# The last two attention turns written out as one sequence with PSUM banks of their own, and the row work of the last three groups placed behind single feed-forward blocks

## The chip, the core and the metric

The kernel runs on one core of a Trainium2 chip. The metric is the time of one execution on the device in microseconds. Five engines work side by side, each with its own queue of instructions: TensorE (PE in the profile, its weight loads PEld), VectorE (DVE), ScalarE (ACT), GpSimd (POOL) and SyncE (SP), which only starts transfers here. They wait for each other through semaphores written by hand. All five queues are written out in the code; no scheduler reorders them.

## The reference, cut to what matters

64 sequences of 128 rows with 256 features go through two layers:

```
x = x + mlstm(layernorm(x), ctx, ctx, gates...)    # 4 heads; decay matrix D from cumulated gates
x = x + einsum('bsi,oi->bso', layernorm(x), ternary(W0) * scale)
x = x + softmax(layernorm(x) @ Wq @ K.T / 16) @ V  # cross attention on ctx
x = x + bitlinear(silu(bitlinear(n, w_gate)) * bitlinear(n, w_up), w_down)   # n = layernorm(x), inner size 1024
# mlstm: C = (q k.T / 8) * D;  h = (C / norm(C)) @ v, then a normalisation over each head
# bitlinear(a, w): each row of a is rounded to 8 bits by its own absolute maximum; w is ternary
```

## The kernel before

**Groups and two phases.** The 64 sequences form `NG` = 16 groups of `GB` = 4. The first phase, called attention here, takes a group through the first three lines of the reference. The second phase is the feed-forward, the fourth line: 64 blocks of one sequence each.

**Attention.** `schedule` writes out turns. In a turn five groups are at different stages: group n is read in and projected, m = n - 1 goes through the mLSTM (to x1), z = n - 2 through the W0 product and the cross attention (x1 to x2 to x3), y = n - 3 gets its layernorm and rounding factors for the feed-forward, and w = n - 4 is rounded to integers and stored to `rows_q` in DRAM. On TensorE the order within a turn is that of `STAGES`. The names used below: DX (decay exponents), QK, T1 (transpose of x1), F0 (x1 times W0), UA and UB (C times v, called U together), T2 (transpose of x2), SC (scores), WT (transpose of the exponentials), O (weights times V). Each use of a stage takes the next of 8 PSUM banks in a ring (`Banks`); `full[k]` and `clear[k]` count the fillings and emptyings of bank k. The last two turns, `NEXT` and `LAST`, have no group to read in: in `NEXT` m = 15, z = 14, y = 13, w = 12; in `LAST` only z = 15, y = 14 and w = 13 are left. On each engine a turn is one call of `turn`, in a fixed order of steps.

**VectorE in these turns.** `cut_product` multiplies QK by D, `statistics(i, ...)` is four bn_stats, four bn_aggr and a variance (i = 1 for x1, 2 for x2, 3 for x3), the head sums end in `hv`, GpSimd raises to the power -1/2 (`power`, and for the heads L993), and VectorE scales the heads and adds x. `row_steps` takes a group's row maxima (`famax`), its scales and the factors `back`.

**Between the phases.** TensorE, ScalarE and GpSimd wait for `phase1`, which VectorE and ScalarE raise behind their last turn. SyncE starts the transposing reads of `rows_q` for blocks 0 to 3 after the store of group 14, and then four loads of x3 (`fx`).

**Feed-forward.** For block i TensorE does gate_up (L640, eight products of 512 columns), then `product_rows` of block i - 2 (L649) and `down` of block i - 3 (L657). ScalarE does Silu (L878), the copy of the transposed rows (L882) and the scaling out (L889). VectorE multiplies (L1327, output C), takes the row maximum (L1330) and two small steps. GpSimd rounds (L1018) and adds x (L1026). `feed_forward` writes out groups 0 to 2 and 11 to 15; groups 3 to 10, that is blocks 12 to 43, are a loop of two passes. The row work of group 15 is done by `last_rows(i)`, single instructions behind single blocks: on VectorE its row maxima behind blocks 6 to 9, scales and factors behind 10 and 11; on ScalarE the normalisation behind 2 to 5 and the rounding behind 48 to 53.

## Time and profile before

| | us |
|---|---|
| median of 3 runs | 716.62 |
| lowest, highest | 715.96, 718.27 |
| the profiled execution | 717.83 |
| its span, first to last instruction | 716.09 |
| mean granted TensorE clock, share of full | 0.973 |

The profile shows one execution. Its time is 1.2 above the median, and 1.7 of it lie outside the span. Times in the text are microseconds from the start of the span. A row gives the start, the length, the engine, the line in the kernel and the tiles; a group of several instructions has one row, and its length is from the start of the first to the end of the last.

### The profile page before, as it was taken

The page shows a single profiled execution, that of the slowest core. Times are in us where ns is not written, and L with a number is a line of the kernel's source. Part 1 is how long each engine was busy: PE and PEld are TensorE (multiplying, and loading weights), DVE is VectorE, ACT ScalarE, POOL GpSimd, SP SyncE. Part 2 cuts the span into 40 slices and gives each one's busy share as a digit, 9 for nine tenths or more (in the row PEclk, how much of TensorE's full clock was granted, in tenths as well). Part 3 has the DMA queues.
Part 4 walks back from the last instruction along what each step waited for, and adds up shares of the span by engine and source line. Part 5 has one row for each costly group of instructions (what it writes and reads, how often), then busy time and mean ns, then how long its engine had stood idle before and what let it go on. Part 6 is the DMA issues. An engine that isn't in the chain of part 4 may idle for free.

```text
span 716.1 us, 15477 instructions
## 1 busy us (share of the span) xinstructions
PE 674.2 (94%) x4914; PEld 518.3 (72%) x4942; DVE 615.9 (86%) x1654; ACT 515.6 (72%) x1171; POOL 376.9 (53%) x554
## 2 busy tenths in 40 slices
PE   4899999999999999999999999987799999999996
PEld 3687887887977878879779788765365666666664
DVE  4697798898898988988988989887699999999994
ACT  3456576777777768777777687665588887888985
POOL 2253464643834645537346455441266666666665
PEclk9969999999999999999999999988699999999999
DMA  8202022022121220320212202005222332424321
GB/s 302 82 1 60 22 68 90 16 90 77 42 90 45 75 89 16 97 89 23 90 45 75 89 16 74 32 15 161 71 82 83 104 114 81 139 81 139 95 78 60
DMA packets 72653, 55.46 MB, mean 77 GB/s; under 512 B 20093, under 2 KB 72318, under 8 KB 72582
## 3 DMA queue, kind: packets, MB, share of 16 engines
q1 hardware_dynamic: 64134, 50.37, 22.6%
q10 hardware_dynamic: 8448, 4.20, 2.0%
q8 instruction: 38, 0.62, 0.4%
q14 instruction: 33, 0.27, 0.1%
HBM read 29.39 MB, written 20.97 MB: 70 GB/s over the span
## 4 chain that ended last, share of the span: by engine, by line
PE 66%; DVE 20%; ACT 9%; issue 3%; DMA 1%; POOL 0%; DVEq 0%; POOLq 0%; ACTq 0%
PE bank L640 10%; PE bank L556 9%; PE bank L586 8%; PE bank L605 8%; PE bank L657 5%; DVE C L1327 4%; PE bank L626 4%; PE bank L462 4%; DVE hmax L1330 4%; ACT ew L851 4%; PE bank L559 3%; PE bank L525 3%; PE bank L649 3%; PE bank L516 2%; PE bank L598 2%
## 5 line engine op out<-in xcount | busy, mean ns | idle before, releaser
L640 PE MATMUL bank<-WGU,fqT 128*128 128x512 bf16 x484 | 124.5, 389 | 6.7 <-DVEq L1304 3.1
L962 POOL TENSOR_SCALAR_AFFINE_SELECT D<-D 128x512 f32<-128x512 f32 x64 | 38.3, 635 | 158.0 <-ACT D L794 158.0
L640 PEld LDWEIGHTS bank<-WGU,fqT 128*128 128x128 bf16 x512 | 48.4, 99 | 61.1 <-DVE C L1327 17.3
L1327 DVE SCALAR_TENSOR_TENSOR C<-bank,fback,D 128x1024 f32<-128x1024 f32 x64 | 82.1, 1283 | 10.3 <-ACT D L878 6.3
L947 POOL TENSOR_TENSOR rs<-ve,minus_half 128x4 f32<-128x4 f32 x64 | 64.2, 1010 | 50.6 <-DVE ve L1072 50.5
L878 ACT ACTIVATE D<-bank,fback 128x1024 f32<-128x1024 f32 x64 | 71.2, 1113 | 19.1 <-PE bank L640 18.9
L1330 DVE TENSOR_REDUCE hmax<-C 128x1 f32<-128x1024 f32 x64 | 78.1, 1220 | 2.2
L882 ACT ACTIVATE fhT<-bank 128x1024 f16<-128x1024 f16 x64 | 65.5, 1023 | 17.0 <-PE bank L649 16.0
L556 PE MATMUL bank<-WX,qcT 128*128 128x268 f32 x256 | 77.3, 426 | 0.0
L1018 POOL TENSOR_SCALAR wtmp<-C,hscale 128x1024 f32<-128x1024 f32 x64 | 71.6, 1118 | 0.2 <-ACT nrm L889 0.2
L1066 DVE BATCH_NORM_STATS2 st<-x 128x6 f32<-128x256 f32 x192 | 67.2, 411 | 2.9
L657 PE MATMUL bank<-WD,fhT 128*128 128x256 f16 x512 | 66.4, 273 | 0.3 <-ACT fhT L882 0.3
L586 PEld LDWEIGHTS bank<-vaug,C 128*128 128x128 f32 x512 | 62.5, 196 | 2.3 <-issue 1.5
L586 PE MATMUL bank<-vaug,C 128*128 128x65 f32 x512 | 62.3, 276 | 1.4 <-DVE C L1165 1.4
L525 PE MATMUL bank<-qcT,GT 128*128 128x512 f32 x128 | 60.2, 594 | 0.7 <-ACT GT L842 0.7
L605 PE MATMUL bank<-W0T,x1T 128*128 128x256 f32 x256 | 59.4, 385 | 0.1
L993 POOL TENSOR_TENSOR hr<-hv,minus_half 128x16 f32<-128x16 f32 x16 | 47.4, 2960 | 18.0 <-DVE hv L1211 18.0
L1011 POOL TENSOR_SCALAR hback<-hstep,mean_abs 128x1 f32<-128x1 f32 x64 | 17.1, 267 | 74.0 <-DVE hscale L1340 65.0
L605 PEld LDWEIGHTS bank<-W0T,x1T 128*128 128x128 f32 x256 | 47.3, 190 | 9.1 <-DVE C L1165 3.0
L805 ACT ACTIVATE qn<-xg,shift,rs 128x256 f32<-128x256 f32 x64 | 33.2, 589 | 27.9 <-POOL shift L954 27.9
L969 POOL TENSOR_TENSOR hh<-us,head_scale 128x256 f32<-128x256 f32 x64 | 43.9, 705 | 15.6 <-ACT usq L779 15.6
L783 ACT ACTIVATE vg<-bank 128x268 f32<-128x268 f32 x64 | 23.5, 389 | 38.4 <-PE bank L559 38.4
(181 smaller groups left out, 1582.0 us busy)
## 6 DMA issues: line engine op xcount, KB each, us to landing
out_dram<-x SPq DMA_DIRECT2D x32, 512.0 KB, 3.1
xg<-in_x_dram SPq DMA_DIRECT2D x16, 512.0 KB, 3.9
cg<-in_ctx_dram SPq DMA_DIRECT2D x16, 512.0 KB, 4.1
rows_q<-fq ACTq DMA_DIRECT2D x16, 256.0 KB, 2.3
xg<-out_dram SPq DMA_DIRECT2D x8, 512.0 KB, 4.3
cg<-out_dram SPq DMA_DIRECT2D x8, 512.0 KB, 4.4
raw<-in_L_ffn_w_gate_dram SPq DMA_DIRECT2D x1, 1024.0 KB, 8.5
x<-in_L_ffn_w_up_dram SPq DMA_DIRECT2D x1, 1024.0 KB, 10.4
```

The lines of the kernel that those rows point to most:

```text
L525: mm = pe.matmul(o[:, :], GT[:, c, rows_at * P:(rows_at + 1) * P], turned[:, EC + c, :, :].rearrange("p b t -> p (b t)"), start=(c == 0), ...
L556: pe.matmul(o[:, 0:VG], qcT[p][:, EC + c, b, :], WX[:, c, :], start=(c == 0), stop=False, skip_group_check=True)
L586: mm = pe.matmul(o[:, h * AUG:(h + 1) * AUG], C[:, b, h, :], vaug[q][:, b, h, :], start=True, stop=True)
L605: mm = pe.matmul(o[:, 0:E], x1T[:, b, c * P:(c + 1) * P], W0T[:, c, :], start=(c == 0), stop=(c == EC - 1))
L640: mm = pe.matmul(ps[k + half], fqT[:, s, c, :], WGU[:, c, which, half * 512:(half + 1) * 512], start=(c == 0), stop=(c == EC - 1))
L657: mm = pe.matmul(o[:, 0:E], fhT[:, s % 2, c * P:(c + 1) * P], WD[:, c, :], start=(c == 0), stop=(c == IC - 1))
L878: act.activation(fsil[:, s % 2, :], gate, ACT.Silu, scale=fback[:, p, s % FB, 0:1]).then_inc(g_clear, 1)
L882: act.activation(fhT[:, s % 2, :], bank_h[s % 2], ACT.Copy, bias=-OFFSET).then_inc(h_clear, 1)
L1018: pool.tensor_scalar(fhr[:, s % 2, :], fh[:, s % 2, :], hscale[:, s % FB:s % FB + 1], CODE, ALU.mult, ALU.add).then_inc(f_hr, 1)
L1066: dve.bn_stats(st[i][:, b, :], src[:, b, :]).then_inc(stats[i], 1)
L1327: dve.scalar_tensor_tensor(out=fh[:, s % 2, :], in0=up, scalar=fback[:, p, s % FB, 1:2], in1=fsil[:, s % 2, :], op0=ALU.mult, op1=ALU.mult ...
L1330: dve.tensor_reduce(hmax[:, s % FB:s % FB + 1], fh[:, s % 2, :], AX.X, ALU.max, apply_absolute_value=True).then_inc(f_hm, 1)
```

## The change

`Banks` is kept for the first 14 turns. For the last two there is `Places`, which gives each stage banks by name, four for group 14's late stages and four for group 15's:

```diff
+def last_places():
+    start = len(FIRST) + len(SECOND) + (NG - 2) * len(BODY)
+    count = [sum(1 for i in range(start) if i % BANKS == k) for k in range(BANKS)]
+    one, two = (3, 4, 5, 6), (7, 0, 1, 2)
+    a = Places({"TB": (5,), "DX": (6, 7, 0, 1), "MB": (2,), "QK": (3, 4, 5, 6), "T1": two, "UA": (3, 4), "UB": (5, 6),
+                "F0": two, "T2": one, "SC": one, "WT": one, "O": one}, count)
+    b = Places({"T1": two, "F0": two, "T2": two, "SC": two, "WT": two, "O": two}, count)
+    return a, b
```

`fore` is the first of the two, `aft` the second. The two turns are gone from `schedule`; behind it each engine has them written out, and `phase1` is gone. x2 and x3 of group 15 have tiles of their own (`x2_last` = hh, `x3_last` = qn), and the feed-forward's banks are others (gate 3 and 4, up 5 and 6, transposes 7 and 0, down 1 and 2). TensorE:

```diff
-            pe.wait_ge(phase1, 2)
+            turn(fore.part("TB", "DX", "MB", "QK", "T1", "UA", "UB", "F0", "T2", "SC"),
+                 None, NG - 1, NG - 2, None, None, 0, NG % 3)
+            turn(aft.part("T1", "F0"), None, None, NG - 1, None, None, 1, (NG + 1) % 3)
+            turn(fore.part("WT"), None, None, NG - 2, None, None, 0, NG % 3)
+            turn(aft.part("T2", "SC"), None, None, NG - 1, None, None, 1, (NG + 1) % 3)
+            turn(fore.part("O"), None, None, NG - 2, None, None, 0, NG % 3)
+            turn(aft.part("WT"), None, None, NG - 1, None, None, 1, (NG + 1) % 3)
+            pe.wait_ge(x3_ready, GB * (NG - 1))
+            gate_up(0, 0, 0)
+            turn(aft.part("O"), None, None, NG - 1, None, None, 1, (NG + 1) % 3)
...
+                    if i == 2:
+                        pe.wait_ge(x3_ready, GB * NG)
```

VectorE (the steps are the old ones as functions), ScalarE and GpSimd:

```diff
+            cut_product(fore, NG - 1, 0)
+            cut_product(fore, NG - 1, 1)
+            statistics(3, x3, NG - 3)
+            head_sums(fore, NG - 1, 1)
+            x2_rows(fore, NG - 2, x2)
+            moved(fore, "F0", GB - 1)
+            statistics(2, x2, NG - 2)
+            heads_out(NG - 1, 1)
+            dve.wait_ge(x1_ready, NG)
+            statistics(1, x1, NG - 1)
+            row_maxima(fore, NG - 2)
+            scales(0, 0)
+            x2_rows(aft, NG - 1, x2_last)
+            moved(aft, "F0", GB - 1)
+            inverse(fore, NG - 2)
+            statistics(2, x2_last, NG - 1)
+            row_maxima(aft, NG - 1)
+            x3_rows(fore, NG - 2, x2, x3)
...
+            turned_copies(fore, "T2", x2T)
+            turned_copies(aft, "T1", x1T)
+            exponentials(fore, NG - 2)
+            turned_weights(fore)
+            turned_copies(aft, "T2", x2T)
+            exponentials(aft, NG - 1)
+            turned_weights(aft)
+            act.preload_act_table_set("silu_and_others")
...
+            head_power(NG - 1)
+            power(2, NG - 2)
+            power(1, NG - 1)
+            power(2, NG - 1)
```

The row work of groups 13, 14 and 15 goes to `last_rows(i)`, behind single blocks. On ScalarE: rounding of 13 behind blocks 7 to 12, normalisation of 14 behind 14 to 17, its rounding behind 24 to 29, the same for 15 behind 31 to 34 and 41 to 46. On GpSimd: power and shifts of 14 behind block 12, of 15 behind block 29. On VectorE:

```diff
+                if i == 0:
+                    inverse(aft, NG - 1)
+                    x3_rows(aft, NG - 1, x2_last, x3_last)
+                for group, src, at in ((NG - 3, None, 1), (NG - 2, x3, 7), (NG - 1, x3_last, 24)):
+                    if src is not None:
+                        if at <= i < at + GB:
+                            row_statistics(src, i - at)
+                        if i == at + GB:
+                            row_variance(group)
+                        at += 11
+                    if at <= i < at + GB:
+                        row_max(group, (i - at,))
+                    if i == at + GB:
+                        row_scales(group)
+                    if i == at + GB + 1:
+                        row_back(group)
```

The feed-forward has no loop any more, and SyncE's order is another:

```diff
-            for g in range(3):
-                static(g)
-            with eng.Fori(0, NG // 4 - 2) as j:
-                for p in range(4):
-                    turn(4 * j + p + 3, (p + 3) % 4, False, False)
-            for g in range(NG - 5, NG):
-                static(g)
+            for g in range(NG):
+                turn(g, g % 4, g == 0, g == NG - 1)
...
             store(NG - 4)
             store(NG - 3)
-            store(NG - 2)
...
+            sp.wait_ge(q_out, 16 * (NG - 3) + 16)
+            for b in range(FB):
+                rows_turned(b, b)
             sp.wait_ge(x1_ready, NG)
             sp.wait_ge(vaug_ready, GB * NG)
+            sp.wait_ge(x_out, 16 * (NG - 2))
             for g in range(4):
                 sp.dma_start(fx[g], grp(out, g)).then_inc(f_in[g], 16)
-            store(NG - 1)
+            store(NG - 2)
+            sp.wait_ge(x3_ready, GB * NG)
+            sp.dma_start(grp(out, NG - 1), x3_last[:, :, :]).then_inc(x_out, 16)
```

TensorE before, from F0 of group 14 (L605) to O of group 15; L586 is U, L598 are T1 and T2, L613 SC, L621 WT, L626 O:

```order
L605 MATMUL bank<-W0T,x1T 128x256 x8
L586 MATMUL bank<-vaug1,C 128x65 x16
L598 MATMUL bank<-ident,x23 128x128 x8
L613 MATMUL bank<-keyT0,x2T 128x128 x8
L621 MATMUL bank<-ident,ew 128x128 x4
L626 MATMUL bank<-vg2,ewT 128x256 x4
L598 MATMUL bank<-ident,x1 128x128 x8
L605 MATMUL bank<-W0T,x1T 128x256 x8
L598 MATMUL bank<-ident,x23 128x128 x8
L613 MATMUL bank<-keyT1,x2T 128x128 x8
L621 MATMUL bank<-ident,ew 128x128 x4
L626 MATMUL bank<-vg0,ewT 128x256 x4
```

The same place after the change; L615 is U, L634 F0, L627 T1 and T2, L642 SC, L650 WT, L655 O, L666 gate_up of block 0:

```order
L615 MATMUL bank<-vaug1,C 128x65 x16
L634 MATMUL bank<-W0T,x1T 128x256 x8
L627 MATMUL bank<-ident,x23 128x128 x8
L642 MATMUL bank<-keyT0,x2T 128x128 x8
L627 MATMUL bank<-ident,x1 128x128 x8
L634 MATMUL bank<-W0T,x1T 128x256 x8
L650 MATMUL bank<-ident,ew 128x128 x4
L627 MATMUL bank<-ident,hh 128x128 x8
L642 MATMUL bank<-keyT1,x2T 128x128 x8
L655 MATMUL bank<-vg2,ewT 128x256 x4
L650 MATMUL bank<-ident,ew 128x128 x4
L666 MATMUL bank<-WGU,fqT 128x512 x8
```

U stands ahead of F0, WT and O of group 14 moved behind T1, F0 and the scores of group 15, and gate_up of block 0 stands ahead of O of group 15.

VectorE before, from the row maxima of the scores of group 15 to its product of block 1 (C):

```order
L1249 TENSOR_REDUCE rawmax<-bank 128x1 x4
L1253 TENSOR_TENSOR negmax<-rawmax,rs2 128x4
L1283 RECIPROCAL einv<-esum 128x4
L1289 SCALAR_TENSOR_TENSOR x23<-bank,einv,x23 128x256 x4
L1066 BN_STATS st3<-x23 128x6 x4
L1069 BN_AGGR mv3<-st3 128x2 x4
L1072 TENSOR_SCALAR ve3<-mv3 128x4
L1309 COPY fback<-back 128x8
L1327 SCALAR_TENSOR_TENSOR C<-bank,fback,D 128x1024
L1330 TENSOR_REDUCE hmax<-C 128x1
L1337 TENSOR_SCALAR hstep7<-hmax 128x1
L1340 RECIPROCAL hscale<-hstep7 128x1
```

And after the change; L1323 writes x3 of group 14 (x23) and of group 15 (qn):

```order
L1298 TENSOR_REDUCE rawmax<-bank 128x1 x4
L1302 TENSOR_TENSOR negmax<-rawmax,rs2 128x4
L1323 SCALAR_TENSOR_TENSOR x23<-bank,einv,x23 128x256 x4
L1470 SCALAR_TENSOR_TENSOR C<-bank,fback,D 128x1024
L1473 TENSOR_REDUCE hmax<-C 128x1
L1480 TENSOR_SCALAR hstep7<-hmax 128x1
L1483 RECIPROCAL hscale<-hstep7 128x1
L1315 RECIPROCAL einv<-esum 128x4
L1323 SCALAR_TENSOR_TENSOR qn<-bank,einv,hh 128x256 x4
L1470 SCALAR_TENSOR_TENSOR C<-bank,fback,D 128x1024
```

x3 of group 15 stands behind block 0, and its statistics are gone from here. They stand, on VectorE after the change, behind blocks 24 to 28; for group 14 behind blocks 7 to 11, of which this is the end (the single behind block 10, block 11, the aggregations behind it, the product of block 12):

```order
L1167 BN_STATS st3<-x23 128x6
L1470 SCALAR_TENSOR_TENSOR C<-bank,fback,D 128x1024
L1473 TENSOR_REDUCE hmax<-C 128x1
L1480 TENSOR_SCALAR hstep7<-hmax 128x1
L1483 RECIPROCAL hscale<-hstep7 128x1
L1172 BN_AGGR mv3<-st3 128x2 x4
L1174 TENSOR_SCALAR ve3<-mv3 128x4
L1470 SCALAR_TENSOR_TENSOR C<-bank,fback,D 128x1024
```

Before, what stands behind blocks 10 and 11 are the scales and factors of group 15, five small instructions.

## Rows read from the trace of the kernel before

**Rows 1.** The page: busy us (share) xinstructions; then the chain by engine.
```profile
PE 674.2 (94%) x4914; PEld 518.3 (72%) x4942; DVE 615.9 (86%) x1654; ACT 515.6 (72%) x1171; POOL 376.9 (53%) x554
...
PE 66%; DVE 20%; ACT 9%; issue 3%; DMA 1%; POOL 0%; DVEq 0%; POOLq 0%; ACTq 0%
```

**Rows 2.** Windows: length, then busy PE, PEld, DVE, ACT, POOL, clock, DMA share, GB/s.
```profile
500.00:520.00 20.00, 15.34 (x63) 6.60 (x65) 13.63 (x29) 10.07 (x12) 5.46 (x9) 0.66 0.29 89
...
640.00:700.00 60.00, 59.55 (x460) 38.87 (x466) 55.65 (x83) 51.39 (x65) 40.66 (x60) 1.00 0.32 95
```

**Rows 3.** The same view in windows of 4 us.
```profile
476.00:480.00 4.00, 2.75 (x12) 1.99 (x10) 3.40 (x13) 2.61 (x9) 2.02 (x1) 0.50 0.00 0
...
508.00:512.00 4.00, 3.08 (x8) 0.98 (x8) 2.82 (x4) 1.95 (x3) 0.16 (x1) 0.50 0.07 16
```

**Rows 4.** The chain from 483 to 513: start, length, engine, output, line, count.
```profile
484.33 1.42 DVE st L1066 x4
...
488.58 1.02 POOL rs L947
...
490.18 2.07 ACT raw L709 x4
...
496.67 1.88 ACT ew L851 x8
...
506.36 1.28 ACT L878
...
508.92 3.58 PE bank L640 x8
```

**Rows 5.** TensorE's timeline: T1, F0 and U, scores, gate_up: start, length, line, tiles.
```profile
451.47 2.02 PE L613 MATMUL bank<-keyT,x2T 128*128 128x128 f32 x16
...
463.73 1.09 PE L598 MATMUL bank<-ident,x 128*128 128x128 f32 x8
464.74 3.69 PE L605 MATMUL bank<-W0T,x1T 128*128 128x256 f32 x16
468.27 3.68 PE L586 MATMUL bank<-vaug,C 128*128 128x65 f32 x32
...
522.00 1.89 PE L640 MATMUL bank<-WGU,fqT 128*128 128x512 bf16 x8
```

**Rows 6.** GpSimd's timeline: head scaling and head power.
```profile
472.86 1.32 POOL L969 TENSOR_TENSOR hh<-us,head_scale 128x256 f32<-128x256 f32 x2
475.12 2.90 POOL L993 TENSOR_TENSOR hr<-hv,minus_half 128x16 f32<-128x16 f32 x1 [0.94 <-DVE hv L1211]
```

**Rows 7.** VectorE's timeline: head products, x1, x2.
```profile
463.54 2.48 DVE L1165 TENSOR_TENSOR C<-bank,D 128x512 f32<-128x512 f32 x4 [0.59 <-POOL D L962]
...
479.62 1.23 DVE L1262 TENSOR_TENSOR x<-xg,hh 128x1024 f32<-128x1024 f32 x1
...
488.42 1.66 DVE L1185 SCALAR_TENSOR_TENSOR x<-bank,rs,x 128x256 f32<-128x256 f32 x4
```

**Rows 8.** VectorE's timeline: products of blocks 1, 2, 6, 12, 27, 28, 44, 63.
```profile
512.53 1.28 DVE L1327 SCALAR_TENSOR_TENSOR C<-bank,fback,D 128x1024 f32<-128x1024 f32 x1 [0.70 <-PE bank L640]
...
515.43 1.28 DVE L1327 SCALAR_TENSOR_TENSOR C<-bank,fback,D 128x1024 f32<-128x1024 f32 x1
...
527.36 1.28 DVE L1327 SCALAR_TENSOR_TENSOR C<-bank,fback,D 128x1024 f32<-128x1024 f32 x1
...
546.43 1.28 DVE L1327 SCALAR_TENSOR_TENSOR C<-bank,fback,D 128x1024 f32<-128x1024 f32 x1
...
593.04 1.28 DVE L1327 SCALAR_TENSOR_TENSOR C<-bank,fback,D 128x1024 f32<-128x1024 f32 x1
...
596.61 1.28 DVE L1327 SCALAR_TENSOR_TENSOR C<-bank,fback,D 128x1024 f32<-128x1024 f32 x1 [0.65 <-issue]
...
646.09 1.28 DVE L1327 SCALAR_TENSOR_TENSOR C<-bank,fback,D 128x1024 f32<-128x1024 f32 x1 [0.18 <-issue]
...
704.02 1.28 DVE L1327 SCALAR_TENSOR_TENSOR C<-bank,fback,D 128x1024 f32<-128x1024 f32 x1
```

More of the change, by code:

```diff
@@ L734, in last_rows, with filled, turned_copies @@
+                if i == 45:
                     whole_rows(NG - 1)
-                if late == GB + 1:
+                if i == 46:
                     store_rows(NG - 1)
+            def filled(bank, stage, i=0):
+                k, value = bank(stage, i)
+                act.wait_ge(full[k], value)
+                return ps[k], clear[k]
+            def turned_copies(bank, stage, dst):
+                for b in range(GB):
+                    o, done = filled(bank, stage, b)
+                    act.activation(dst[:, b, :], o[:, 0:E], ACT.Copy).then_inc(done, 1)
@@ new lines, in key_copy, with products_out @@
+            def key_copy(bank, stage, dst):
+                o, done = filled(bank, stage)
+                act.activation(dst, o[:, :], ACT.Copy).then_inc(done, 1)
+            def products_out(bank, stage):
+                for b in range(GB):
+                    if half(b)[0] != stage:
+                        continue
+                    o, done = filled(bank, *half(b))
+                    v = o[:, 0:NH * AUG].rearrange("p (h d) -> p h d", h=NH)
+                    act.activation(us[:, b, :, :], v, ACT.Copy)
+                    act.activation(usq[:, b, :, :], v[:, :, 0:DH], ACT.Square).then_inc(done, 1)
@@ L1000, in turn, with last_rows @@
                                            mean, ALU.subtract).then_inc(vaug_ready, 1)
-                if m is None and z is not None:
-                    power(3, z)
-                    shifts(3, z)
             schedule(pool, turn)
+            cut(fore, 0)
+            cut(fore, 1)
+            power(1, NG - 2)
+            power(3, NG - 3)
+            shifts(3, NG - 3)
+            for b in range(GB):
+                scale_heads(fore, b)
+            head_power(NG - 1)
+            power(2, NG - 2)
+            power(1, NG - 1)
+            power(2, NG - 1)
+            def last_rows(i):
+                for group, at in ((NG - 2, 12), (NG - 1, 29)):
+                    if i == at:
+                        power(3, group)
+                        shifts(3, group)
             def scale_back(i, s):
@@ new lines, in inverse, with x3_rows @@
+            def inverse(bank, z):
+                moved(bank, "SC", GB - 1)
+                dve.reciprocal(einv[:, :], esum[:, :]).then_inc(inved, 1)
+                dve.wait_ge(inved, z + 1)
+            def x3_rows(bank, z, src, dst):
+                if 0 < z < NG - 1:
+                    dve.wait_ge(x_out, 16 * z)
+                for b in range(GB):
+                    o, done = filled(bank, "O", b)
+                    dve.scalar_tensor_tensor(out=dst[:, b, :], in0=o[:, 0:E], scalar=einv[:, b:b + 1],
+                                             in1=src[:, b, :], op0=ALU.mult, op1=ALU.add).then_inc(done, 1)
+                moved(bank, "O", GB - 1)
+                dve.sem_inc(x3_ready, GB)
@@ L1181, in turn @@
                 if z is not None:
-                    dve.wait_ge(rstd[1], z + 1)
-                    for b in range(GB):
-                        o, done = filled("F0", b)
-                        dve.scalar_tensor_tensor(out=x2[:, b, :], in0=o[:, 0:E], scalar=rs[1][:, b:b + 1],
-                                                 in1=x1[:, b, :], op0=ALU.mult, op1=ALU.add).then_inc(done, 1)
-                    moved("F0", GB - 1)
+                    x2_rows(bank, z, x2)
+                    moved(bank, "F0", GB - 1)
                     statistics(2, x2, z)
@@ L1295, in turn @@
                     statistics(1, x1, m)
-                if m is None and z is not None:
-                    statistics(3, x3, z)
                 if isinstance(n, int) and n == 0:
```

352 lines of the change are left out of this document (183 added, 169 removed).

## The prediction, made before the changed kernel was run

> **What bounds the kernel now.** I read the page first, then windows by stage, then the chain of waits and the timelines of the stretch that the change rewrites. TensorE is busy for 94% of the span and holds 66% of the chain [rows 1]. That average hides one bad stretch. In the feed-forward (640 to 700) TensorE is busy for 59.55 of 60 us at the full clock, with VectorE behind it at 55.65; between 500 and 520 it is busy for 15.34 of 20 us at a mean granted clock of 0.66 [rows 2]. The last two attention turns run from about 461 to 502 with nothing of a third group to fill the gaps. TensorE idles, and its clock falls to 0.50 (1.2 GHz of 2.4): in 476 to 480, after it had waited for the copies of x2, and again until past 508 [rows 3]. The chain shows what is late: statistics, a power on GpSimd, the normalisation of rows on ScalarE, a score stage at half clock, the exponentials, a table load of 1.28, and a first block whose eight remaining products take 3.58 [rows 4] where eight take 1.89 at full clock [rows 5]. So two parts can be costed apart: the way from 461 to block 2 of the feed-forward, whose first VectorE product starts at 515.43, and blocks 2 to 63, which end with the product at 704.02 [rows 8]. What follows 704.02 (12.1 us of drain) is the same code in both.
>
> **Part 1, x1 of the last group comes earlier.** VectorE's four products of group 15 run from 463.54 in 2.48 us [rows 7], so the first two batches have theirs by 464.8. Before, TensorE then does the feed-forward-0 product F0 (464.74, 3.69) and only after it U (468.27, 3.68) [rows 5]. Now U comes first: 464.9 to 468.5. VectorE then makes the head sums before x2 and not behind it. Two statistics take from 484.33 to the power at 488.58 [rows 4], so 2.1 each; products end at 466.0, statistics of group 13 at 468.1. The head sums ended 3.2 behind U before (471.95 to the head power at 475.12 [rows 5, 6]), so now at 471.7. GpSimd must still do the power and shifts of group 13 (1.6, from 488.58 to 490.18 in its like [rows 4]), to 469.8, and four head scalings (1.32 for two [rows 6]), to 472.4. The head power of 2.90, which started at 475.12 [rows 6], starts at 472.5. x1, which was ready at 479.62 + 1.23 = 480.85 [rows 7], is ready 2.6 earlier, at 478.2.
>
> **Part 2, from x1 to block 2.** Before, VectorE adds x3 of group 14 and takes its statistics ahead of group 15's x2, and ScalarE puts 2.07 of normalisation ahead of the x2 copies [rows 4]. Both go. The new way, all at full clock: T1 1.09 and F0 3.69 [rows 5] from 478.3 give 483.0; statistics of x1 (2.1) and the power (1.02) end at 481.4 beside it. The last quarter of x2 (1.66 for four [rows 7]) ends at 483.5. T2's last quarter with its copy (about 0.7) and the scores (2.02 [rows 5]) end at 486.2, but statistics 2 (2.1) and their power (1.0) end at 486.9, so the row maximum's product is done at 487.1. Exponentials 1.88 [rows 4]: 489.0. One transposition and gate_up(0), 0.2 + 1.89 [rows 5]: 491.1. ScalarE copies the transposed weights meanwhile, then from about 490.0 comes the table load of 1.28, to 491.3: it used to start only when the first gate product was there, now most of it lies behind the products. Silu (508.92 less 506.36 less 1.28, about 1.2 [rows 4]): VectorE's product of block 0 at 492.6. VectorE's block takes 2.9 (512.53 to 515.43 [rows 8]); in block 0 it has x3 of group 15 behind it, four instructions like the x2 ones [rows 7] and a reciprocal, 1.8. So block 1 at 497.3 and block 2 at 500.2. The O products and gate_up(1), 2.02 + 1.89, lie beside VectorE's 4.7. Ideal gain: 15.2.
> The clock takes some of it back. TensorE is idle from about 475 to 478.3, where x1 is awaited, and again for some 2 us in block 1. It fell after gaps of that size in the trace, so I expect it low for a part of F0 and for a part of the first blocks. The bounds: nothing; or half clock throughout, which adds 4.7 (T1, F0) + 2.3 (scores) + 1.9 (gate_up(0)) = 8.9, and 2.0 beyond VectorE's cover in block 0. I take 2.2, a quarter of that, since in the nearest window with such a gap (476 to 480) TensorE worked 2.75 us at half clock [rows 3], which costs 1.4, and there are about one and a half such places. Block 2 then starts at 502.4, **13.0 earlier**.
> The Trainium skill, "ScalarE: Activation LUTs", section on what ACT_TABLE_LOAD costs, states a load of about 1283 ns and a drain of about 1380 ns more. The trace has the Silu right behind the load and no such drain; by the page block 0 would come 1.4 later and the result would be 706.6, by the row it is what the sum says.
>
> **Part 3, blocks 2 to 63.** Before: 704.02 - 515.43 = 188.59. The last 19 steps, 646.09 to 704.02, are written out and take 3.049 each [rows 8]; they are TensorE's 3.05 (522.00 to the next block's first product [rows 5] is 1.73 + 0.45 + 0.87) and already carry one ScalarE set (four row scalings, whole rows, store) at no visible price. Three things change.
> First, the loop goes. Its 32 blocks, 546.43 to 646.09, take 3.114 each, with one step of 3.57 (593.04 to 596.61) at the branch back [rows 8]. Written out they cost 3.049: 2.1 saved. Base for 61 steps: 186.0.
> Second, row maxima, scales and factors of a group stand behind six single blocks. Before that is so for group 15 alone: 527.36 to 546.43 [rows 8] is 19.07 against 6 x 3.049 = 18.29, so 0.8: VectorE's 2.9 plus 0.3 is only 0.1 over TensorE. Now there are three such sets: 2.3.
> Third, statistics of groups 14 and 15 also stand there, four singles and then four aggregations with the variance. A single takes 0.35 of VectorE (1.42 for four [rows 4]), like a row maximum, so 4 x 0.1; the aggregation adds the other 0.7 of a statistic to one block, 2.9 + 0.7 = 3.6, so 0.55. About 0.95 a set, two sets: 1.9. The bounds: 0, if TensorE's buffers cover it, and 2.1 a set, if nothing does. GpSimd's power and shifts (1.4) in blocks 12 and 29 lie beside some 1.0 of its free time a block (40.66 of 60 busy [rows 2]) and a product that is wanted two blocks later: nothing. ScalarE's extra 0.5 a block stays under 3.05, and whole rows (1.05) fall twice on a block that VectorE stretches anyway: nothing.
> Sum: 186.0 + 2.3 + 1.9 = 190.2, **1.6 longer**.
> The queues: on SyncE the transfers of transposed rows now go ahead of the four loads and of both stores; they need only the rows of group 12, which ScalarE stores behind its copies of U, at about 469.5. Behind them, the store of group 15 waits for x3 (497.3), and the transposition for block 4 is queued behind it. That block begins near 505, so some 7 us are left for it.
> The Trainium skill, "Runtime: NRT & Kernel Launch", section on instruction fetch, says that a taken branch out of the window being fetched stalls, while straight code is streamed ahead. By that alone only the step at the branch is saved, 0.5 and not 2.1, which would give 706.8; the rows show 0.05 to 0.1 in every block of the loop as well.
>
> **Sum.** The span of 716.1 becomes 716.1 - 13.0 + 1.6 = 704.7. The profiled execution took 717.83, 1.7 beyond its span; the median of the runs shown is 716.62, 1.2 under that one execution. I take the difference of 11.4 from the median: **705.2**.
>
> **Rivals.** (a) The statistics pieces lie fully on the path: 2 x 2.1 - 1.9 = 2.3 more, 707.5, and if row maxima do so as well (3 x 2.3 - 2.3 = 4.6) 712.1. So the row work would only have moved. Against the second half: blocks 6 to 11 show 0.1 a block [rows 8]. (b) The clock stays low through most of the merged turns: 8.9 of Part 2 instead of 2.2, 711.9. For: three falls in 40 us before. Against: F0, scores and O of two groups now stand closer. (c) The slower end: the same, but the clock also stays low in the feed-forward's first blocks. Then the way to block 2 costs 8.9 + 2.0 instead of 2.2, 713.9, and each block at half clock 3.05 more. One block gives 717.0 and is where it turns; two give 720. Against: from 508 to 512 the clock was low with TensorE busy, and block 2 still came 2.9 behind block 1 [rows 3, 8]. (d) The new order does not lift group 15 off VectorE's queue: if the row maxima of group 14 (behind statistics of x1) or its x3 rows delay group 15 by their whole 1.1 + 1.7, 708.0.
>
> **How the numbers follow.** Forecast, 702 to 707.4: 0.55. (a) 0.12, (b) 0.12, (d) 0.08, (c) 0.05; 0.08 is left for a clock that costs nothing and covered statistics (down to 705.2 - 2.2 - 1.9 = 701.1). The range 701.3 to 711.9 leaves out (c), the far half of (a) and the edge of (b). A measurement of this kernel tells 0.3% (2.1 us) from no change. Faster needs 714.5 or less: all but (c), 0.93 with some doubt taken off; within 0.3%: 0.04; slower: 0.03.
>
> **What would show it.** In the changed profile: x1 of group 15 near 478; VectorE's first block product near 493 to 495, its third near 502; the table load beside products of gate_up(0); a granted clock of 0.5 for 3 to 7 us near F0, and not for 14; steps of 3.05 in plain blocks, 3.15 beside a single piece, 3.6 at the two aggregations; blocks 2 to 63 in about 190. Wrong would be: half clock past block 4, a step of over 3.3 beside a single piece, or plain blocks over 3.1.

## The result and the profile after

| | before | after |
|---|---|---|
| median of 4 runs each | 716.75 us (715.96 to 718.27) | 706.72 us (705.16 to 709.16) |
| ratio after to before | | 0.9846, 95% interval 0.9823 to 0.9869 |
| profiled execution, its span | 717.83, 716.1 | 705.16, 703.2 |
| time outside that span | 1.7 | 2.0 |

The changed kernel is 1.5% faster. The forecast was 705.2 in a range of 701.3 to 711.9. Its sign, its size and its likeliest case held; the steps did not all hold, and two of them erred in opposite directions.

The page of the changed kernel, which answers to [rows 1] (busy us, share, instructions; then the chain by engine):

```profile
PE 663.5 (94%) x4942; PEld 511.3 (73%) x4942; DVE 616.5 (88%) x1660; ACT 512.4 (73%) x1171; POOL 378.8 (54%) x554
...
PE 65%; DVE 22%; ACT 8%; issue 2%; DMA 1%; POOL 1%; POOLq 0%; DVEq 0%; ACTq 0%
```

TensorE's share is 94% in both: 10.7 us of its busy time went (663.5 for 674.2) with 12.9 of the span. Hardly any work was removed. Its busy time fell because more of the same products ran at the full clock. Not all of that is the change's doing: 3.7 of the 10.7 lie in the first 72 us (54.70 busy for 58.44), where both do the same work and the low clock differs from one execution to the next.

Windows of the changed kernel (length; busy PE, PEld, DVE, ACT, POOL with counts; granted clock; DMA share; GB/s), the first the answer to [rows 2]:

```profile
500.00:520.00 20.00, 20.00 (x154) 12.86 (x153) 19.31 (x39) 15.74 (x19) 11.53 (x18) 0.96 0.15 39
...
475.00:480.00 5.00, 2.63 (x20) 2.30 (x20) 4.61 (x15) 1.20 (x4) 1.97 (x2) 1.00 0.14 28
480.00:485.00 5.00, 4.94 (x30) 4.20 (x30) 4.51 (x19) 3.62 (x17) 1.02 (x1) 1.00 1.02 336
...
498.00:502.00 4.00, 3.25 (x15) 1.76 (x16) 3.86 (x8) 0.47 (x1) 1.35 (x2) 0.57 0.57 166
```

500 to 520 is full feed-forward now. Between 475 and 485 the clock stays at 1.00 although TensorE is idle for nearly half of the first 5 us; only 498 to 502 has a low stretch (0.50 for most of it).

TensorE's timeline of the merged turns (start, length, line, tiles; in brackets idle time before and what ended it), beside [rows 5]:

```profile
464.32 3.76 PE L615 MATMUL bank<-vaug,C 128*128 128x65 f32 x32 [0.15 <-DVE C L1263]
467.91 3.67 PE L634 MATMUL bank<-W0T,x1T 128*128 128x256 f32 x16
...
478.35 1.06 PE L627 MATMUL bank<-ident,x 128*128 128x128 f32 x8 [2.37 <-DVE x L1311]
479.33 3.69 PE L634 MATMUL bank<-W0T,x1T 128*128 128x256 f32 x16
...
484.51 2.02 PE L642 MATMUL bank<-keyT,x2T 128*128 128x128 f32 x16
...
489.46 1.89 PE L666 MATMUL bank<-WGU,fqT 128*128 128x512 bf16 x8
```

U is first (L615), F0 of group 14 behind it (L634); the one wait of size is 2.37 for x1 of group 15. VectorE and ScalarE of the same stretch, beside [rows 7, 8, 4]:

```profile
462.88 2.48 DVE L1263 TENSOR_TENSOR C<-bank,D 128x512 f32<-128x512 f32 x4 [0.59 <-POOL D L1034]
...
476.98 1.23 DVE L1311 TENSOR_TENSOR x<-xg,hh 128x1024 f32<-128x1024 f32 x1
...
487.11 0.16 DVE L1302 TENSOR_TENSOR negmax<-rawmax,rs 128x4 f32<-128x4 f32 x1 [0.26 <-POOL rs L1019]
...
492.50 1.28 DVE L1470 SCALAR_TENSOR_TENSOR C<-bank,fback,D 128x1024 f32<-128x1024 f32 x1 [3.62 <-ACT D L951]
...
489.96 1.28 ACT L945 ACT_TABLE_LOAD   x1
491.25 1.11 ACT L951 ACTIVATE D<-bank,fback 128x1024 f32<-128x1024 f32 x1
```

The last product of row maxima starts at 487.11; the table load lies beside gate_up(0); Silu follows it at once; block 0 has its VectorE product at 492.50. VectorE's later block products start at 497.41 (block 1), 500.68 (2), 533.39 (12), 633.37 (44) and 691.29 (63).

**Where the time went.** Read from one mark to the next: the head products of group 15 start 0.66 earlier (462.88 for 463.54), before anything that differs here has run. Nearly all of it, 0.59, is there at the first head products of all, after first and before second:

```profile
35.14 2.47 DVE L1263 TENSOR_TENSOR C<-bank,D 128x512 f32<-128x512 f32 x4
...
35.73 2.47 DVE L1165 TENSOR_TENSOR C<-bank,D 128x512 f32<-128x512 f32 x4
```

Up to 36 us the granted clock is 1.00 in both, so this is the start of the execution and not the clock; what makes it differ is not known. From the head products of group 15 to block 2 it is 37.80 for 51.89: **14.09 saved**. Blocks 2 to 63 are 190.61 for 188.59: **2.02 lost**. From block 63 to the end it is 11.9 for 12.1. Together 0.66 + 14.09 - 2.02 + 0.2 = 12.9, the difference of the spans. The medians differ by 10.0 and not by 12.9: the other three runs of after have spans of 707.2, 706.1 and 703.4, two of them longer at a lower mean clock (0.984 and 0.990 for 0.993), so the profiled execution is the shortest of four. The 14.09 belongs to these two executions as well. In the kernels with plain reads, described next, the same way takes 50.86 before and 39.47 after, 11.39 less.

### The profile page after: what moved, and what is told of

It reads as the page before. It is cut to its first block, busy times and chain, and to the rows that moved or that the text cites. A ratio compares the mean times of both kernels' runs of the same rounds, so it can differ in the third digit from the quotient of the medians.

```text
span 703.2 us, 15197 instructions
## 1 busy us (share of the span) xinstructions
PE 663.5 (94%) x4942; PEld 511.3 (73%) x4942; DVE 616.5 (88%) x1660; ACT 512.4 (73%) x1171; POOL 378.8 (54%) x554
## 4 chain that ended last, share of the span: by engine, by line
PE 65%; DVE 22%; ACT 8%; issue 2%; DMA 1%; POOL 1%; POOLq 0%; DVEq 0%; ACTq 0%
PE bank L666 11%; PE bank L585 9%; PE bank L634 8%; PE bank L615 7%; PE bank L683 5%; PE bank L655 4%; DVE C L1470 4%; ACT ew L822 4%; PE bank L491 4%; DVE hmax L1473 4%; PE bank L554 3%; PE bank L588 3%; PE bank L675 3%; PE bank L627 2%; PE bank L545 2%
## 5 line engine op out<-in xcount | busy, mean ns | idle before, releaser
L666 PE MATMUL bank<-WGU,fqT 128*128 128x512 bf16 x512 | 125.0, 382 | 4.8 <-DVE C L1470 4.4
L666 PEld LDWEIGHTS bank<-WGU,fqT 128*128 128x128 bf16 x512 | 48.1, 98 | 57.7 <-DVE C L1470 17.9
L585 PE MATMUL bank<-WX,qcT 128*128 128x268 f32 x256 | 74.0, 412 | 0.0
L1109 POOL TENSOR_SCALAR wtmp<-C,hscale 128x1024 f32<-128x1024 f32 x64 | 71.6, 1119 | 0.2 <-issue 0.2
L1157 DVE BATCH_NORM_STATS2 st<-x 128x6 f32<-128x256 f32 x180 | 63.1, 412 | 2.6
L615 PEld LDWEIGHTS bank<-vaug,C 128*128 128x128 f32 x512 | 61.6, 194 | 2.6 <-issue 1.9
L615 PE MATMUL bank<-vaug,C 128*128 128x65 f32 x512 | 61.6, 274 | 1.5 <-DVE C L1263 1.5
L634 PE MATMUL bank<-W0T,x1T 128*128 128x256 f32 x256 | 59.4, 385 | 0.0
L634 PEld LDWEIGHTS bank<-W0T,x1T 128*128 128x128 f32 x256 | 47.3, 190 | 9.0 <-DVE C L1263 3.0
L683 PEld LDWEIGHTS bank<-WD,fhT 128*128 128x128 f16 x512 | 47.4, 98 | 4.9 <-issue 0.6
```

The source lines that it names most:

```text
L585: pe.matmul(o[:, 0:VG], qcT[p][:, EC + c, b, :], WX[:, c, :], start=(c == 0), stop=False, skip_group_check=True)
L615: mm = pe.matmul(o[:, h * AUG:(h + 1) * AUG], C[:, b, h, :], vaug[q][:, b, h, :], start=True, stop=True)
L634: mm = pe.matmul(o[:, 0:E], x1T[:, b, c * P:(c + 1) * P], W0T[:, c, :], start=(c == 0), stop=(c == EC - 1))
L666: mm = pe.matmul(ps[k + half], fqT[:, s, c, :], WGU[:, c, which, half * 512:(half + 1) * 512], start=(c == 0), stop=(c == EC - 1))
L683: mm = pe.matmul(o[:, 0:E], fhT[:, s % 2, c * P:(c + 1) * P], WD[:, c, :], start=(c == 0), stop=(c == IC - 1))
L1109: pool.tensor_scalar(fhr[:, s % 2, :], fh[:, s % 2, :], hscale[:, s % FB:s % FB + 1], CODE, ALU.mult, ALU.add).then_inc(f_hr, 1)
```

## The experiments

The edited kernels read the stored rows of the feed-forward plainly into `fqT` instead of transposing them on the way, so their feed-forward multiplies rows that lie the wrong way round; sizes and counts of the instructions stay. before_rows and after_rows have only that edit, and they are what the others are compared with. All were timed beside the kernel before (716 to 718 us in each set). The marks stand up to 2.7 us apart from one profiled execution to another before the code that differs has run, so stretches are compared, not places.

### A plain read in place of the transposing one, in both kernels

```diff
-                sp.dma_start_transpose(fqT[:, s, :, :], rows_q[b, :, :]).then_inc(x_turned[s], 16)
+                sp.dma_start(fqT[:, s, :, :], rows_q[b, :, :].rearrange("s (c p) -> s c p", c=EC)).then_inc(x_turned[s], 16)
```

> The kernel before, with one thing changed that all kernels named rows or made from them share: the 64 reads of the rounded rows from DRAM into fqT are plain transfers and not transposing ones, so the feed-forward multiplies rows that lie the wrong way round; sizes and counts of all instructions stay. It is the measure for the kernels made from the kernel before. Both theories: within 1.5 of 716.7, since SyncE and these transfers were waited for nowhere but at the very start of the feed-forward.

> The changed kernel with plain reads instead of the transposing ones; the measure for the kernels made from the changed one. Both theories: within 1.5 of 706.7, 10 below before_rows, its runs spread over some 4 us; if the clock in the merged turns is what varies, the runs with the lower mean clock are the longer ones.

before_rows: median 717.56 (716.47 to 718.66, 12 runs), ratio to before 1.0012 (0.9995 to 1.0028). Blocks 2 to 63 take 188.62, as they did (188.59). after_rows: 706.65 (705.61 to 707.61, 6 runs), ratio 0.9861 (0.9836 to 0.9885); blocks 2 to 63 take 190.61, to the hundredth what after takes. So how the rows are read costs nothing in either, and the edit is a sound base for the rest. The way from the head products to block 2 is another matter, since the clock falls in it or not: 50.86 in before_rows and 50.78 in before_written for 51.89 in before, and 39.47 in after_rows for 37.80 in after.

The profile of after_rows also shows what that of after did not: half clock during F0 of group 15. Window and TensorE's timeline of after_rows, then VectorE's x1 and block 0:

```profile
480.00:484.00 4.00, 4.00 (x13) 3.21 (x12) 2.70 (x15) 2.58 (x11) 1.02 (x1) 0.57 0.94 292
...
479.05 1.06 PE L627 MATMUL bank<-ident,x 128*128 128x128 f32 x8 [2.37 <-DVE x L1311]
480.02 5.38 PE L634 MATMUL bank<-W0T,x1T 128*128 128x256 f32 x16
...
477.68 1.23 DVE L1311 TENSOR_TENSOR x<-xg,hh 128x1024 f32<-128x1024 f32 x1
...
494.88 1.28 DVE L1470 SCALAR_TENSOR_TENSOR C<-bank,fback,D 128x1024 f32<-128x1024 f32 x1 [3.62 <-ACT D L951]
```

F0 takes 5.38 and not 3.69, behind the same wait of 2.37. From the start of x1 to block 0 it is 17.20, against 15.52 in after. The code there is the same, F0 alone is 1.69 longer, and so **1.7 between them is the clock**. The profile of var_moved, an experiment below that differs from after_rows only from block 11 on, shows the fall too: F0 takes 5.38 behind a wait of 2.36.

### The loop of the feed-forward written out, nothing else

before_rows with this edit:

```diff
-            for g in range(3):
-                static(g)
-            with eng.Fori(0, NG // 4 - 2) as j:
-                for p in range(4):
-                    turn(4 * j + p + 3, (p + 3) % 4, False, False)
-            for g in range(NG - 5, NG):
+            for g in range(NG):
                 static(g)
```

> before_rows with all 16 groups of the feed-forward written out and nothing else. Theory of the prediction (every block of the loop costs 0.065 more than a written-out one, and the branch back 0.5): blocks 12 to 43 take 97.6 instead of 99.7 us, 2.1 less than before_rows. Rival 1 (only the branch back costs): 0.5 less. Rival 2 (written-out code is fetched late): not less.

Median 716.31 (713.85 to 717.94, 12 runs), ratio 0.9993 (0.9975 to 1.0010), so against before no gain in time is shown. Blocks 2 to 63 take 186.44 against 188.62 in before_rows: 2.18 less, of which 2.08 lie in blocks 12 to 44, where the loop was (97.60 for 99.68). The median of the spans is 2.7 lower (713.1 for 715.8), but that of the times only 1.25: outside the span this kernel spends 3.1 us (2.1 to 4.7), before_rows 1.7 or 1.8 in every run. After, with the loop gone too, spends 2.0 in all four; of the 22 runs of the edited kernels made from it 17 spend 1.9 to 2.5 and five 3.0 to 4.0. So the step of the prediction holds inside the span, and in the time of this kernel a half of it was given back at the start or end of the execution, by something that no profile shows. Its cause stays open.

### The variance taken one product later

after_rows with the instruction that makes the variance (L1174) moved from the end of the four aggregations to a place behind the next block's product and row maximum, in blocks 12 and 29:

```diff
                 for b in range(GB):
                     dve.bn_aggr(mv[3][:, b, :], st[3][:, b, :]).then_inc(aggr[3], 1)
-                dve.wait_ge(aggr[3], GB * group + GB)
-                dve.tensor_scalar(ve[3][:, :], mv[3][:, :, 1], LN_EPS, 1.0, ALU.add, ALU.mult).then_inc(veps[3], 1)
...
                     ffn_mul(i, s, g, p % 2)
+                    late_variance(i)
                     row_scale(i, s)
```

What it is aimed at stands in the profile of after. The steps from block 11 to 12 and from 28 to 29 are 4.19 and 4.18, where the prediction had 3.6. VectorE and GpSimd of after around block 12:

```profile
532.03 0.36 DVE L1172 BATCH_NORM_AGGREGATE mv<-st 128x2 f32<-128x6 f32 x4
532.42 1.06 DVE L1174 TENSOR_SCALAR ve<-mv 128x4 f32<-128x4 f32 x1
533.39 1.27 DVE L1470 SCALAR_TENSOR_TENSOR C<-bank,fback,D 128x1024 f32<-128x1024 f32 x1
...
532.11 0.26 POOL L1102 TENSOR_SCALAR hback<-hstep,mean_abs 128x1 f32<-128x1 f32 x1 [1.11 <-DVE hscale L1483]
532.34 1.12 POOL L1109 TENSOR_SCALAR wtmp<-C,hscale 128x1024 f32<-128x1024 f32 x1
```

An instruction on four numbers a row takes 1.06 us. Its like takes 0.17 in an attention turn. It starts 0.08 behind GpSimd's rounding of the block (L1109) and ends with it (533.48 and 533.46).

> after_rows, and the small VectorE instruction that makes the variance of x3 (L1174, 1.06 us in block 11, while GpSimd rounds; 0.17 elsewhere) moved from behind the aggregations to behind the next block's row maximum, where GpSimd is idle. Theory A (it waits for GpSimd's instruction, as if the two shared a way into the memory): it takes 0.17 there, the steps from block 11 to 12 and from 28 to 29 fall from 4.19 to 3.3, blocks 2 to 63 take 1.2 to 1.8 less. Theory B (the aggregations and their chain are simply long, 0.7 as in the prediction, and the row's length is a reading of the profiler): nothing changes, each of the two steps keeps 0.8 or more over 3.3, or hands it to the next.

Steps 11 to 12 and 28 to 29 fall to 3.24 and 3.13; blocks 2 to 63 take 188.68 for 190.61, **1.93 less**. VectorE and GpSimd of that kernel:

```profile
536.84 1.28 DVE L1474 SCALAR_TENSOR_TENSOR C<-bank,fback,D 128x1024 f32<-128x1024 f32 x1
538.16 1.22 DVE L1477 TENSOR_REDUCE hmax<-C 128x1 f32<-128x1024 f32 x1
539.29 0.16 DVE L1178 TENSOR_SCALAR ve<-mv 128x4 f32<-128x4 f32 x1
...
537.82 0.72 POOL L1117 TENSOR_TENSOR x<-nrm,cg 128x256 f32<-128x256 f32 x1
539.76 0.26 POOL L1102 TENSOR_SCALAR hback<-hstep,mean_abs 128x1 f32<-128x1 f32 x1 [1.22 <-DVE hscale L1487]
```

The same instruction takes 0.16 where GpSimd has nothing under way. The median does not show the gain: 707.38 (703.96 to 708.75, 6 runs) against 706.65. In the profiled execution the head products came 2.0 later (465.53 for 463.58), which takes all of it, and for another reason: 1.2 of it is there at the first head products (37.28 for 36.09), with the clock still at 1.00, and the rest comes between 57 and 68 us, with half clock from 55.6 to 62.5. The shortest span is 701.9, against 703.6 in after_rows, but the median of the spans is 705.35 against 704.0, and six runs don't tell such a spread from a gain of 1.9. So the 1.93 is shown between the marks, and not in the time.

### Pairs of instructions, measured alone

A kernel of its own, which computes nothing of the reference: in each round VectorE runs one row maximum of 256 and then one small instruction, once with GpSimd idle and once beside its rounding of 128x1024.

```diff
+                if big:
+                    pool.tensor_scalar(wtmp[:, :], fh[:, :], sc[:, 0:1], 1.0, ALU.mult, ALU.add).then_inc(step, 1)
...
+                dve.tensor_reduce(rmax[:, 1:2], xt[1][:, 0, :], AX.X, ALU.max)
+                if form == 0:
+                    i = dve.tensor_scalar(ve[:, :], mv[:, :, 1], LN_EPS, 1.0, ALU.add, ALU.mult)
```

> A kernel of its own that only measures pairs of instructions (its output is a copy of x): in 72 rounds VectorE takes a row maximum of 256 elements and then one small instruction of six kinds in turn, once with GpSimd idle and once while GpSimd runs the rounding instruction of the feed-forward (128x1024, 1.12 us). Theory A (a small VectorE instruction with two operands or of the scalar kind waits for GpSimd's instruction to end): the variance's tensor_scalar, the tensor_tensor and the other tensor_scalar take 0.17 alone and 0.5 to 0.8 beside it; reciprocal, row maximum and bn_stats take the same in both. Theory B (the long rows of the changed kernel have another cause): all six are the same in both.

| VectorE's instruction | alone | beside GpSimd's 1.12 |
|---|---|---|
| tensor_scalar, 4 a row, like the variance | 0.16 | 0.74 |
| tensor_tensor, 16 a row, both from SBUF | 0.17 | 0.74 |
| tensor_scalar, 16 a row | 0.17 | 0.75 |
| reciprocal, 4 a row | 0.17 | 0.17 |
| row maximum of 256 | 0.41 | 0.41 |
| bn_stats of 256 | 0.42 | 0.42 |

The first form and the fourth in its timeline:

```profile
72.54 0.16 DVE L183 TENSOR_SCALAR ve<-mv 128x4 f32<-128x4 f32 x1
...
72.95 1.12 POOL L163 TENSOR_SCALAR wtmp<-fh,sc 128x1024 f32<-128x1024 f32 x1
...
73.35 0.74 DVE L183 TENSOR_SCALAR ve<-mv 128x4 f32<-128x4 f32 x1
...
79.78 1.12 POOL L163 TENSOR_SCALAR wtmp<-fh,sc 128x1024 f32<-128x1024 f32 x1
...
80.18 0.17 DVE L189 RECIPROCAL he<-hn 128x4 f32<-128x4 f32 x1
```

The tensor_scalar ends at 74.09, GpSimd's rounding at 74.07; the reciprocal inside the same rounding is untouched. The small instruction doesn't run slower, it waits until GpSimd's has ended, and only some kinds do. The Trainium skill, "SBUF — State Buffer", section "Who interferes with whom", says that the port pair shared by VectorE and GpSimd is "an exclusive lock", that a tensor_scalar in a 2-port mode and an instruction with two SBUF inputs contend with GpSimd for it, and that tensor_reduce never does; the table agrees in every form that the section names. It doesn't name reciprocal or bn_stats.

Not every instruction of GpSimd holds VectorE up. The experiment tried only the rounding. In the kernel before, VectorE makes the scales of a group while GpSimd is in the head power, which runs from 475.12 for 2.90 [rows 6]:

```profile
476.21 0.17 DVE L1111 TENSOR_SCALAR fscale<-famax 128x4 f32<-128x4 f32 x1
```

A tensor_scalar on four numbers a row is untouched there (and at 363.83 in an earlier turn as well). So the lock of the page does not show beside the power. What sets the power apart from the rounding and the head scaling was not tested.

### F0 of group 14 put back ahead of U

after_rows with one entry of the merged turns moved. It undoes the cause that the prediction names for x1. In that call F0 is that of group 14 and U that of group 15; the expectation on record calls it F0 of the last group and speaks of F0 behind T1, which is not what the edit touches: T1 and F0 of group 15 stand where they stood.

```diff
-            turn(fore.part("TB", "DX", "MB", "QK", "T1", "UA", "UB", "F0", "T2", "SC"),
+            turn(fore.part("TB", "DX", "MB", "QK", "T1", "F0", "UA", "UB", "T2", "SC"),
```

> The same plain reads, and in the merged turns F0 of the last group is put back in front of U, as it stood before the change; all else as in after_rows. It undoes the cause that the prediction names for the first 2.6 us: U first, hence head sums, head scalings and x1 earlier. Theory A: from VectorE's head products to the start of x1 16.1 us pass, as in the kernel before (14.1 in after_rows and after), x1 comes 2.0 later than in after_rows at an equal start, blocks 2 to 63 stay at 190.6, and the median is 0.5 to 2.6 higher than 706.65; less than 2.0 only if TensorE, which then no longer has F0's 3.7 behind T1, gives some back. Rival: x1 is bound by the statistics on VectorE and the powers on GpSimd whichever product goes first; then x1 comes less than 1.0 later and the median stays within 0.7. A third outcome: F0 has then lain beside the head work, TensorE goes from T1 straight to the scores, and the order is worth nothing in the end.

Median 709.21 (707.05 to 711.55, 6 runs), ratio 0.9886 (0.9864 to 0.9907): 2.6 above after_rows (the intervals of the two ratios overlap), in the median of the spans 1.65 above (705.65 for 704.0). VectorE's marks, the head power on GpSimd and TensorE's wait for x2 of group 14:

```profile
463.49 2.48 DVE L1263 TENSOR_TENSOR C<-bank,D 128x512 f32<-128x512 f32 x4 [0.60 <-POOL D L1034]
...
479.35 1.22 DVE L1311 TENSOR_TENSOR x<-xg,hh 128x1024 f32<-128x1024 f32 x1
...
474.52 2.90 POOL L1046 TENSOR_TENSOR hr<-hv,minus_half 128x16 f32<-128x16 f32 x1 [1.17 <-DVE hv L1292]
...
474.98 1.94 PE L627 MATMUL bank<-ident,x 128*128 128x128 f32 x8 [3.09 <-DVE x L1270]
```

From head products to x1 it is 15.86, against 14.10 in after_rows and in after (expected by the theory: 16.1; by its rival: under 15.1). The order of these two products is worth **1.76** of the way to block 2, and the third outcome, that it is worth nothing in the end, falls too: in this profile T1, F0 and the scores of group 15 run at full clock, block 0 follows x1 in 15.52 as in after, and from the head products to block 2 it is 39.55 for 37.80 in after. Against after_rows, whose profile has the 1.7 of low clock during F0, nothing is left of the order (39.55 for 39.47); blocks 2 to 63 take 190.82. The clock was low here from 474.0 to 480.9, from the end of the wait of 3.09 for x2 on, over products of T2 and the scores that x1 doesn't wait for.

### TensorE's wait for x1 filled

after_rows with nine products of 512 columns that nobody reads, behind the scores of group 14:

```diff
+            def warm(o, times):
+                for _ in range(times):
+                    pe.matmul(o[:, :], WGU[:, 0, 0, 0:P], WGU[:, 0, 0, 0:512], start=True, stop=True)
...
+                                if z == NG - 1 and b == 0:
+                                    warm(o, 9)
```

> After with plain reads of the stored rows in place of the transposing transfers (as in after_rows; the feed-forward so multiplies untransposed rows), and with nine more 512-column products of TensorE put where it waits for x1 of group 15. Nobody reads them; at full clock they take 1.94 us of a wait of 2.37. It tests what brings TensorE's clock down behind that wait. Theory C: the idle wait does. In after_rows the clock was half from 480.4 to 483.8, during F0, and from the start of x1 to VectorE's product of block 0 17.2 us passed, against 15.5 in the profiled execution of after, in which it did not fall there. So with the wait filled: no half clock between 475 and 490, 15.5 us from x1 to block 0, and a median 1.0 to 1.7 below after_rows (706.65), 705.0 to 705.7. Theory D: the fall there is not due to the wait. Then half clock of some 3.4 us is seen between 475 and 490 as in after_rows, x1 to block 0 takes 17.2, and the median stays within 0.5 of 706.65. If the nine products come late and delay T1, x1 to block 0 grows by their overhang, under 0.5.

Median 706.22 (705.64 to 708.06, 4 runs), ratio 0.9849 (0.9826 to 0.9872): 0.4 under after_rows. TensorE in that profile, and the window around F0:

```profile
476.17 2.10 PE L472 MATMUL bank<-WGU 128*128 128x512 bf16 x9
478.60 1.09 PE L633 MATMUL bank<-ident,x 128*128 128x128 f32 x8 [0.33 <-DVE x L1317]
479.60 3.69 PE L640 MATMUL bank<-W0T,x1T 128*128 128x256 f32 x16
...
480.00:484.00 4.00, 3.88 (x21) 3.27 (x20) 3.47 (x16) 2.56 (x13) 1.02 (x1) 1.00 0.94 306
```

The wait is down to 0.33, F0 takes 3.69 at full clock, no half clock stands anywhere from there to block 63, and x1 to block 0 is 15.45: what the theory of the idle wait said. It isn't shown for all that. The profile of after has the wait unfilled and no fall behind it either, the spans here (703.3, 706.1, 703.4, 704.3) are hardly shorter than those of after_rows (705.5, 703.9, 703.6, 704.0, 705.6, 704.0), and the median moved by the 0.4 that the other theory allows. What can be said: after the same wait of 2.37 the clock fell in two profiled executions (after_rows, var_moved) and not in a third (after), the fall costs 1.7, and filling the wait gains too little to see. Which wait brings it down, and when, is left open.

## Why the prediction was right, and where it was not

**The sum.** The span: 703.2, forecast 704.7. The median: 706.72, forecast 705.2. The likeliest case (702 to 707.4) holds, and none of the rivals came true as a whole. That the span came within 1.5 is luck in part. The clock term of 2.2 did not come in the profiled execution and the start was 0.66 early; against that x1 gained 0.6 less than forecast, the way from x1 to block 2 was 0.5 longer than at full clock in the forecast, and blocks 2 to 63 took 0.4 more. The result is made of two stretches, so each is set against its forecast.

**Part 1, x1: the place was met by chance.** x1 was ready at 478.21, forecast 478.2, but the head products had started 0.66 earlier for another reason. From them to x1 it was 14.10 for 16.08: 2.0 earlier and not 2.6. The cause was right, since f0_first2 takes 1.76 of these 2.0 away. Of the missing 0.6, half is in front of the head power: measured from the head products it starts at 9.27, forecast 472.5 - 463.54 = 8.96. There all four head sums take 0.60 instead of 0.17, each while GpSimd scales a head; before, only the first two did. GpSimd has the scalings done at 471.62 and then waits 0.53 for `hv`, so this is on the path. The other half is behind it: from the head power to x1 is 4.83 for 4.50, since VectorE has statistics of x2 ahead of the product with it. VectorE of after:

```profile
469.14 0.60 DVE L1278 SCALAR_TENSOR_TENSOR hn<-us 128x16 f32<-128x16 f32 x1
469.78 0.59 DVE L1281 TENSOR_TENSOR he<-hn,thr 128x16 f32<-128x16 f32 x1
470.40 0.61 DVE L1284 TENSOR_SCALAR hn<-he 128x16 f32<-128x16 f32 x1
471.05 0.60 DVE L1286 SCALAR_TENSOR_TENSOR he<-hn 128x16 f32<-128x16 f32 x1
471.69 0.17 DVE L1290 TENSOR_TENSOR hsum<-hvar,he 128x16 f32<-128x16 f32 x1
...
475.72 1.23 DVE L1308 TENSOR_TENSOR hh<-hh,hr 128x1024 f32<-128x1024 f32 x1
...
469.01 2.61 POOL L1040 TENSOR_TENSOR hh<-us,head_scale 128x256 f32<-128x256 f32 x4
```

**Part 2, to block 2: right but for the clock term and one row maximum.** Each mark that was forecast up to block 1 came within 0.4: F0 ended at 483.0, the scores at 486.5 (486.2), the product of row maxima came at 487.11 (487.1), the exponentials ended at 489.2 (489.0), gate_up(0) at 491.35 (491.1), the table load at 491.24 (491.3), block 0 at 492.50 (492.6), block 1 at 497.41 (497.3). Block 2 came at 500.68, 14.09 earlier when the start is aligned, forecast 13.0 with the clock and 15.2 without. The step from block 1 to 2 was 3.27 where 2.9 was forecast. Half clock stood in 498.2 to 501.6, but it isn't the cause: in filled_wait2, with full clock there, the step is 3.23. VectorE has one more instruction in it, the first row maximum of group 13:

```profile
500.31 0.41 DVE L1207 TENSOR_REDUCE famax<-raw 128x1 f32<-128x256 f32 x1
```

The change puts it behind block 1; the prediction counted all six steps of that set in blocks 2 to 63 and took the bare 2.9 here. So of the clock term of 2.2 next to nothing came in this execution. In after_rows 1.7 came, all at F0; a second low stretch at block 1 (500.8 to 504.2) left that step at 3.27 too. A single number for it was the wrong form. It is a cost that comes in some executions and not in others; that the median of 706.72, 1.6 above the profiled execution, holds a part of it is likely and not shown. The places at which the forecast looked for it (near F0, and in block 1) were right, though only the first costs time; the "3 to 7 us" near F0 were 0 in the profile of after and 3.4 in that of after_rows. Silu stood right behind the table load (489.96 + 1.28 and 491.25), so the drain of some 1.4 that the Trainium skill, "ScalarE: Activation LUTs", adds in its section on what ACT_TABLE_LOAD costs did not come, as it had not before.

**Part 3, blocks 2 to 63: 190.61, forecast 190.2.** Its terms:

- The loop: 2.18 by before_written, forecast 2.1. The loop cost something in each of its blocks, and not at the branch alone (0.5): in before_rows the 31 steps without the one at the branch (3.58) took 3.10 in the mean, written out all 32 took 3.05.
- The pieces of row work: steps beside a single piece took 3.13 to 3.23, most of them 3.15 as forecast; none passed 3.3. From block 41 on the steps without a piece took 3.04 in the mean. One of them, from block 45 to 46, took 3.50, and the blocks around it made that up (18.29 for the six from 41 on).
- The two aggregations: **the term that was mis-sized**. Forecast 3.6 a step, 0.55 over a plain one; measured 4.19 and 4.18, 1.14 over. The 0.7 was taken from a statistic in an attention turn, where GpSimd does nothing beside it. Here the aggregations took 0.36 as there, but the variance waited for GpSimd's rounding and took 1.06. The prediction asked of GpSimd only whether it had time for its own added work, and not what it does to VectorE's. var_moved puts the price of this at 1.93 in the two sets; without it the two steps are 0.19 and 0.08 over a plain one, less than the 0.55.
- The rest came out lower in turn: from before_written's 186.44 to 190.61 is 4.17, of which 1.93 is that wait; 2.24 are left for two more sets of row maxima and the statistics without it. Forecast were 1.6 + 1.9 = 3.5 in all. A part is made up right behind a set: the six blocks from 12 on took 18.01 and not 18.29. In var_moved they took 18.03, so that isn't an answer to the long step.

Of rival (a), that the row pieces lie fully on the path, the variance is a true case and the single pieces are not: it cost 0.4 over the forecast and not 2.3. (b) and (c), a clock low through the turns or into the feed-forward, are out: the clock was 1.00 from 475 to 485, TensorE was busy for 20.00 of 20 us from 500 to 520 at 0.96, and where the clock did fall at F0 it cost 1.7 and not 8.9. (d), group 15 delayed behind group 14 on VectorE by the row maxima or the x3 rows, did not come: VectorE waits 0.28 for F0 before the last quarter of group 15's x2 (483.06). Statistics of group 14's x2 cost the 0.3 behind the head power.

**Outside the span** the forecast carried 1.7 over unchanged; it was 2.0 for after, up to 4.0 in some runs of the kernels made from it, and 3.1 for the kernel with the loop alone written out. Nothing in the prediction covers that.

## What to carry to other kernels

When a small instruction is moved from one stage to another, its duration must be read again in the new company: ask what GpSimd runs at that moment, and which kinds of VectorE's instructions wait for it, before a price from elsewhere is used. Compare stretches between marks of the same work rather than places in the span, or a shift that comes from elsewhere makes a step look met that was not. A clock that falls in some executions belongs in the range as a cost that is there or not, and one profile of after doesn't say which.

## What the runs showed of the chip that was not expected

- A tensor_scalar, or an instruction with two inputs from SBUF, on 4 or 16 numbers a row ended only with GpSimd's rounding or head scaling under way: 0.74 or 0.75 for 0.16 or 0.17 in the pairs, 1.06 in the feed-forward, 0.60 four times beside the head scalings. Reciprocal, row maximum and bn_stats took the same beside the rounding as alone, and beside GpSimd's head power of 2.90 a tensor_scalar took 0.17.
- After the same wait of 2.37 us TensorE's clock fell to 0.50 for 3.4 us in two profiled executions and stayed at 1.00 in a third. F0 took 5.38 or 3.69, and block 0 came 1.7 later or not. Another fall of the same length, at block 1, cost 0.04.
- A loop of 32 blocks written out saved 2.18 us in blocks 2 to 63, and that kernel spends 1.3 more outside the span. The changed kernel, where more than the loop differs, spends 0.3 more there. The cause is not known.
